# Value moments on ScalarE, routing rows split and sent later, and new orders in three queues of a fused attention and mixture-of-experts kernel

## The reference

```
x = x + mixing(layernorm(x), k, skip, ctx)    # mixing, per row pair (i, j) of a head block of 8 rows:
#   kv = v_i * x2_j ;  y = causal_conv(kv, k_head) + kv * skip_i ;  out_j = sum_i y_ij * x1_i   (x1 = x2 = ctx)
x = x + ffn(layernorm(x))
#   ffn: scores = sigmoid(xf @ gate.T); top 2, weights normalised, times 2.5
#   shared = (silu(xf @ sg.T) * (xf @ su.T)) @ sd.T     (hidden width 704)
#   routed = sum over the 2 experts of weight * ((silu(xf @ eg.T) * (xf @ eu.T)) @ ed.T)   (hidden width 352)
```

## Time and profile before

| | |
|---|---|
| median of 3 runs | 714.75 us (713.62 to 715.01) |
| the profiled execution | 712.94 us, of which the trace spans 710.9 us |
| TensorE busy | 654.9 us, 92% of the span |
| VectorE, ScalarE, GpSimd busy | 447.6, 294.1, 352.3 us |
| mean granted TensorE clock | 0.979 |

### The profile page before, as it was taken

The page is one execution under the profiler, slowest core; times in us unless marked ns, Lnnn a source line. Parts: engine busy times, 40 slices in busy tenths (PEclk is TensorE's granted clock), DMA queues, the critical chain, the costliest instruction groups (busy, mean ns, idle before and its releaser), DMA issues.

```text
span 710.9 us, 11541 instructions
## 1 busy us (share of the span) xinstructions
PE 654.9 (92%) x3475; PEld 330.8 (47%) x3476; DVE 447.6 (63%) x720; ACT 294.1 (41%) x374; POOL 352.3 (50%) x294
## 2 busy tenths in 40 slices
PE   5979878977999999899999998996999999999993
PEld 3534334433444444344444443444555555555551
DVE  5999988876987695988896778873432111221110
ACT  5356679333233643233541277623433332323321
POOL 2999899926676355685565006400132223222322
PEclk9999999999899999999999999999999999999998
...
GB/s 206 289 108 116 93 89 148 23 50 48 107 102 92 177 30 16 101 65 62 88 30 125 256 177 304 353 149 171 224 167 130 131 125 137 132 133 124 143 73 58
DMA packets 130519, 91.57 MB, mean 129 GB/s; under 512 B 96992, under 2 KB 110816, under 8 KB 129952
## 3 DMA queue, kind: packets, MB, share of 16 engines
...
q10 hardware_dynamic: 576, 0.82, 0.5%
...
## 4 chain that ended last, share of the span: by engine, by line
PE 55%; DVE 15%; POOL 10%; ACT 8%; issue 4%; DMA 3%; SPq 3%; POOLq 0%; DVEq 0%; ACTq 0%
PE banks L809 16%; PE banks L810 16%; PE banks L811 16%; POOL arena L655 7%; DVE mixT L1462 2%; PE banks L901 2%; DVE arena L1455 2%; DVE stats L1468 2%; POOL arena L712 1%; PE banks L905 1%; PE banks L906 1%; POOL arena L683 1%; DMA arena<-split_filters 1%; DVE silu L1497 1%; DVE hm L1602 1%
## 5 line engine op out<-in xcount | busy, mean ns | idle before, releaser
L655 POOL TENSOR_TENSOR arena<-arena 128x512 f32<-128x512 f32 x120 | 140.4, 1200 | 58.8 <-ACT arena L1155 31.5
L772 POOL DMA_INDIRECT out<-xf,ids x39 | 60.7, 1557 | 183.5 <-DMA out<-xf,ids 130.1
L809 PE MATMUL banks<-arena 128*128 128x512 f16 (+1 forms) x330 | 124.9, 379 | 16.9 <-DVE arena L1455 13.0
L810 PE MATMUL banks<-arena 128*128 128x512 f16 (+1 forms) x330 | 124.9, 379 | 0.0
L811 PE MATMUL banks<-arena 128*128 128x512 f16 (+1 forms) x330 | 124.9, 378 | 0.0
L809 PE MATMUL banks<-arena,normed 128*128 x312 | 97.5, 313 | 0.0
L810 PE MATMUL banks<-arena,normed 128*128 x312 | 97.5, 313 | 0.0
L811 PE MATMUL banks<-arena,normed 128*128 x312 | 97.5, 313 | 0.0
L1817 DVE SCALAR_TENSOR_TENSOR hm<-banks,silu 128x256 f32<-128x256 f32 x39 | 16.5, 424 | 117.3 <-PE banks L811 98.9
L1115 ACT ACTIVATE arena<-arena 128x2048 f16<-128x2048 f32 x31 | 59.0, 1904 | 70.8 <-POOL arena L655 68.1
L1455 DVE TENSOR_TENSOR arena<-banks,arena 128x512 f32<-128x512 f32 x128 | 80.4, 681 | 11.7 <-PE banks L811 11.5
...
## 6 DMA issues: line engine op xcount, KB each, us to landing
...
```

The lines of the kernel that those rows point to most:

```text
L655: nc.gpsimd.tensor_tensor(kv[s % 2][:, lb * COLS:(lb + 1) * COLS].rearrange("p (b j i) -> p b j i", i=NH, j=NH), v[:, a, None, :].to_broad ...
L772: nc.gpsimd.indirect_dma_start(out=out, out_offset=bass.IndirectOffsetOnAxis(ap=ids[slot][:, 0:1], axis=0), in_=yg[slot], in_offset=None, ...
L809: nc.tensor.matmul(dst, wh, xh, start=(k == 0), stop=False)
L810: nc.tensor.matmul(dst, wh, xl, start=False, stop=False)
```

## The change

Edits, by queue:

1. **Value moments** leave VectorE. ScalarE makes them with its accumulator: four Copy instructions (scale -1/L) for minus the mean, four Square instructions (bias minus the mean) for the variance. `value_root` on GpSimd does three instructions of 128x4 (scale and add, power, product). `values` on ScalarE reads new tiles for scale and bias.
2. **Head 11's low part** goes from VectorE to GpSimd.
3. **GpSimd's order in group 1**: `outer` 10 to 13 and low parts 10, 11, 12 come in a block, pieces 6 and 7 behind low part 12.
4. **Pair rows**: `pairs` is split in `pair_ranks` (next to head 6) and `pair_rows` (head 7). `send_rows(g-2)` goes behind `outer(s0+2)` of group g, instead of the end of group g-1; the last but one is sent behind the loop.
5. **ScalarE's order**: filter 11 is turned ahead of `feed_norm(0)`, high part 12 after the shared pieces; in groups 1 and 2 `gated` stands ahead of `high_parts` at h=6; `values` between the two parts of `gated(.., 2)`.
6. **VectorE's order in group 1**: two tiles of `mixed(0)` ahead of `products(8)`, the other two behind `total(8)`, and the rest interleaved.
7. **SyncE**: filter 13 is loaded ahead of the rows of group 2; in the tail the first four `load_ids` go ahead of the loads of expert 6, and the loads of experts 6 and 7 come one tile later.
8. **Tail**: in the last group's hidden tiles VectorE's pieces of experts 1 and 3 are spread over m=1 to 4 (`between`), ScalarE does `gated_high` first and its two pieces behind, waiting for expert 1's low parts; `pieces_behind` moves one tile later for most pieces.
9. **TensorE**: in group 2 both halves of `prepare(3)` stand behind head 21.

```
-DVE_LOWS = (0, 1, 3, 5, 6, 7, 8, 9, 11) + tuple(range(2 * HG - 2, H, 2))
+DVE_LOWS = (0, 1, 3, 5, 6, 7, 8, 9) + tuple(range(2 * HG - 2, H, 2))
...
-        pieces_behind = {1: [(6, 0), (6, 1)], 2: [(6, 2)], 3: [(6, 3)]} | {c + 4: [(7, c)] for c in range(EX_PARTS)}
+        between = {1: [(1, 2), (1, 3)], 2: [(3, 0), (3, 1)], 3: [(3, 2)], 4: [(3, 3)]}
+        loads_behind = {1: (6, 2), 2: (6, 3), 3: (7, 0), 4: (7, 1), 5: (7, 2), 6: (7, 3)}
+        pieces_behind = {1: [(6, 0), (6, 1)], 3: [(6, 2)], 4: [(6, 3)]} | {c + 5: [(7, c)] for c in range(EX_PARTS)}
...
# SyncE, g == 1
                 load_filter(s0 + 4)
                 if g == 1:
+                    load_filter(s0 + 5)
                     sp.wait_ge(shared_l, 7)
# SyncE, tail
             load_tile(3, 3)
+            for t in range(RING):
+                load_ids(t, t)
             load_expert(6, 0, 1)
...
                 if t == 0:
-                    for u in range(RING):
-                        load_ids(u, u)
                     sp.wait_ge(base_ready, Q * G)
...
-                if t < 2:
-                    load_expert(6, t + 2)
-                elif t < 2 + EX_PARTS:
-                    load_expert(E - 1, t - 2)
+                if t in loads_behind:
+                    load_expert(*loads_behind[t])
...
# GpSimd
+            def value_root(g):
+                pool.wait_ge(value_square_ready, Q * g)
+                nc.gpsimd.tensor_scalar(value_var[:], value_square[:], 1 / L, EPS, ALU.mult, ALU.add
+                                        ).then_inc(value_var_ready, 1)
+                pool.wait_ge(value_var_ready, g)
+                nc.gpsimd.tensor_tensor(value_rstd[:], value_var[:], minus_half[:], ALU.pow).then_inc(value_rstd_ready, 1)
+                pool.wait_ge(value_rstd_ready, g)
+                nc.gpsimd.tensor_tensor(value_shift[:], value_mean[:], value_rstd[:], ALU.mult).then_inc(v_shift_ready, 1)
...
-                    low_parts(s0 + h)
+                    if g == 1 and h < 4:
+                        if h == 0:
+                            outer(s0 + 2)
+                            piece(5)
+                            outer(s0 + 3)
+                            inverse_root(1)
+                            low_parts(s0 + 2)
+                            low_parts(s0 + 3)
+                            outer(s0 + 4)
+                            outer(s0 + 5)
+                            low_parts(s0 + 4)
+                            piece(6)
+                            piece(7)
+                        continue
+                    if g != 1 or h > 4:
+                        low_parts(s0 + h)
...
                     if s0 + h + 2 < H:
                         outer(s0 + h + 2)
+                    if g > 1 and h == 0:
+                        send_rows(g - 2)
                     if g == 0 and h == 2:
-                        inverse_root(1)
+                        value_root(1)
                     elif g > 0 and h == 1:
-                        inverse_root(2 * g)
-                    elif 0 < g < G - 1 and h == (5 if g == 1 else 4):
-                        inverse_root(2 * g + 1)
+                        inverse_root(g)
+                    elif 0 < g < G - 1 and h == 5:
+                        value_root(g + 1)
...
-                else:
-                    send_rows(g - 1)
-            inverse_root(2 * G - 1)
+            send_rows(G - 2)
+            inverse_root(G)
...
# ScalarE
+            def value_moments(g):
+                act.wait_ge(x_in[g], 32)
+                act.wait_ge(skip_ready, Q * g)
+                act.wait_ge(tokT_ready, Q * g)
+                for q in range(Q):
+                    nc.scalar.activation(normed[:, q, :], x_tok[g % 3][:, q, :], ACT.Copy, scale=-1 / L,
+                                         accum_out=value_mean[:, q:q + 1]).then_inc(value_mean_ready, 1)
+                act.wait_ge(value_mean_ready, Q * g)
+                for q in range(Q):
+                    nc.scalar.activation(normed[:, q, :], x_tok[g % 3][:, q, :], ACT.Square, bias=value_mean[:, q:q + 1],
+                                         accum_out=value_square[:, q:q + 1]).then_inc(value_square_ready, 1)
...
# ScalarE, h == 5 and h == 6 of groups 1 and 2
                         turn_filter(s0 + h + 1)
-                        if g == 1:
-                            values(g + 1)
+                        gated_silu(g - 1, 2)
+                        values(g + 1)
+                        gated_high(g - 1, 2)
                         high_parts(s0 + h + 2)
-                        gated(g - 1, h - 3)
...
                         turned(g + 1, range(2, Q))
+                        gated(g - 1, h - 3)
                         high_parts(s0 + h + 2)
-                        gated(g - 1, h - 3)
...
                         gated(g - 1, h - 3)
-                        if 1 < g < G - 1 and h == 4:
-                            values(g + 1)
+                        if 0 < g < G - 1 and h == 4:
+                            value_moments(g + 1)
...
# VectorE, g == 1
+                    mixed_tile(0, 0)
+                    mixed_tile(0, 1)
+                    products(s0, 0, g)
+                    dve.wait_ge(outT_ready, Q)
+                    total(s0, 0)
+                    mixed_tile(0, 2)
+                    mixed_tile(0, 3)
+                    mixed_moments(0)
+                    mixed_moments(0, True)
+                    products(s0 + 1, 1, g)
+                    mixed_shift(0)
+                    total(s0 + 1, 1)
+                    feed_low(0, range(0, 2))
+                    products(s0 + 2, 2, g)
+                    feed_low(0, range(2, Q))
+                    total(s0 + 2, 2)
...
-                    if h == (6 if g < G - 1 else 4):
+                    if g == G - 1 and h == 4:
                         pairs(g - 1)
+                    elif g < G - 1 and h == 6:
+                        pair_ranks(g - 1)
+                    elif g < G - 1 and h == 7:
+                        pair_rows(g - 1)
```

114 lines of the change are left out of this document (55 added, 59 removed).

## The result

The changed kernel takes 723.26 us (median of 4, 721.39 to 725.05), the kernel before in the same session 714.88 us (median of 4, 713.62 to 716.54). The ratio is 1.0116 with a 95% interval of 1.0082 to 1.0149: slower by 1.2%. The forecast was 707.3 us, with a range of 699.5 to 716 us.

What follows compares the result with a forecast made beforehand. The prediction took TensorE, busy 92% of the span, to bound the kernel, so only closing its gaps or keeping its clock up pays. Nine terms summed to -7.4 us, from the median 714.75 to 707.3 us, range 699.5 to 716.

Steps and rivals of the forecast that it cites:

- 1 group 0: Group 0: convolve(3) starts sooner without VectorE's moments, but GpSimd's queue gives the gain back; 0 us (-1.3 to +1.6).
- 2 front of group 1: Group 1 up to convolve(13): one gap moves to convolve(10), another goes, later work slips; -0.7 us (-3 to +2).
- 3 rest of group 1: Group 1 from convolve(13): earlier values and silu(0,3) close gaps and low clock, pair_rows costs some; -9.3 us (-12 to -5).
- 4 entry of group 2: Entry of group 2: row transfers ahead of low part 17, outer(19) and the root delay the root; +4.2 us (+1 to +7).
- 5 inside of group 2: Inside group 2: gaps at convolve(20), near 286 us and at 301.2 us go; -3.4 us (-3.4 to 0).
- 6 entry of group 3: Entry of group 3: root 4 us later, but meets some 3 us of spare time; +1 us (0 to +3).
- 7 last hidden tiles: Last hidden tiles: later silu(3,2) and pieces between products make down(3,0) wait for VectorE; +3.7 us (0 to +4.5).
- 8 hidden layer of tile 1: Transfer at 496.7 us: ids and a load leave the queue between turns, so the wait goes; -7.0 us (-7.0 to -4).
- 9 ahead of tile 9: Ahead of tile 9: VectorE's 28th piece comes a tile later, TensorE waits; +3.3 us and +0.8 for the clock.
- Dear moments: Rival: ScalarE's accumulating instructions take 1.3 us each, with activation table loads; +4.6, 719.4 us, slower; chance 0.13.
- The root behind the transfers: Rival: the late root makes the entries of groups 2 and 3 cost 7 and 5 us; -0.6, 714.2 us; chance 0.10.
- more is gained: Rival: last-hidden-tiles and tile 9 costs are hidden, group 1's first gaps close too; -14, 700.7 us; chance 0.19.

Runs made afterwards that it cites:

- e16: e9 with var_eps in a two-operand form and pair rows behind products(15) and its total in groups 1 and 2; 710.43 us.
- e11: Changed kernel with the row transfers in two halves around the root, behind outer(19); 733.41 us.
- e15: e9 with var_eps in a two-operand form and low part 17 ahead of the row transfers in GpSimd's queue; 714.30 us.
- e18: Changed kernel with VectorE's add_shared(0) ahead of the second half of the moments in groups 2 and 3; 718.52 us.
- e9: Changed kernel with group 1's front, last hidden tiles and last pieces as before, and expert loads one tile earlier, ids kept ahead; 711.03 us.
- e6: Changed kernel with the front of group 1 (queue orders, low part 11, filter 13) as before; 717.20 us.
- e8: Changed kernel with ScalarE's high part 16 (24) ahead of silu(0,3) in head 6 of groups 1 and 2, as before; 730.09 us.
- e5: Changed kernel with pair ranks and pair rows together in head 6 and row transfers at the end of the group, as before; 722.03 us.
- e7: Changed kernel with the value moments back on VectorE, every queue order as changed; 733.27 us, ratio 1.0228.
- e3: Changed kernel with SyncE's order behind the tiles and the places of the pieces of experts 6 and 7 as before; 720.46 us.
- e4: Changed kernel with expert loads one tile earlier and last pieces in their old places, ids still ahead of the first turn; 717.06 us.

## Why the prediction was wrong

Its terms against the starts of TensorE, in us:

| term | forecast | trace | |
|---|---|---|---|
| 1 group 0 | 0 | -0.6 | right |
| 2 front of group 1 | -0.7 | +3.4 | outside its bounds |
| 3 rest of group 1 | -9.3 | -8.1 | right |
| 4 entry of group 2 | +4.2 | +6.4 | size within bounds, cause wrong for TensorE |
| 5 inside of group 2 | -3.4 | +0.5 | outside its bounds |
| 6 entry of group 3 | +1 | +2.3 | within bounds |
| 7 last hidden tiles | +3.7 | +4.4 | right |
| 8 hidden layer of tile 1 | -7.0 | -7.2, then +5.6 | first half came |
| 9 ahead of tile 9 | +4.1 | +5.6 | right, within bounds |
| sum (forecast) and start of tile 10 (trace) | -7.4 | +12.4 | |

- **The step that failed is what pair rows and the other small instructions around the root cost on VectorE (terms 4 to 6: +1.8 forecast, +9.2 found).** I took pair rows at the 3.5 us that they last before, as +0.8 us once in group 1, and put the entry down to the root behind the transfers. The runs show that VectorE's small instructions last as long as GpSimd lets them: pair rows 2.3 us beside an idle GpSimd (e16), 5.5 beside `outer`, 9.0 beside `outer` and a low part (e11, e15); var_eps 0.17 us beside an idle one (e11) and 2.7 to 5.2 us beside a run in group 2. The end of `pick(1)` went from 0.85 to 3.3 us the same way. The change moved work on GpSimd to just these places. The root did come late: the transfers took 15.9 us instead of 13.6, the root ended 27.1 us behind `outer(18)` instead of 23.2, and VectorE waited 1.84 us for it where it waited 0 before. But no gap of TensorE above 0.9 us follows from that; the one at `down(0,2)` stands ahead of it, behind var_eps. How much of the 9.2 us is VectorE's held instructions is not isolated: moving `add_shared` out from behind var_eps returned 1.8 us at `convolve(17)` (e18), and every kernel that left GpSimd idle beside one of the two places paid elsewhere. Why a small instruction stays held over several of GpSimd's is not shown; in group 3 var_eps was held for one only, 1.06 us in the changed kernel and 1.03 us in e9, with three more of GpSimd's behind.
- **Term 2** named each wait and mis-sized their sum. I had the gap move to `convolve(10)` at about the size of the one it replaced; it is 4.04 us and brings 5.3 us at the low clock with it, and filter 12, issued behind the transposes, lands at 121.5 us, so that low part 12 and the two pieces come late on GpSimd. e6 puts the whole at 5.2 us, the later kernels at 3.4 to 6.5.
- **Term 3** held by its place and size. Without the order in head 6 the stretch loses 4.9 us (e8), without pair rows in head 7 5.0 us (e5), without ScalarE's moments 1.7 us (e7; the forecast gave them 0.9 us). That the order pays only with pair rows in head 7 was not in the forecast, which counted pair rows as a cost alone. The moments are worth more elsewhere: e7 is 4.1 us late already at `convolve(13)` and 11.0 us at the start of group 3.
- **Term 5** forgot pair rows in group 2 (1.74 us at `convolve(24)`), and the gap at `convolve(20)`, which it had go, is 1.95 us. The step that failed fails here too: the moments left VectorE, and the small instructions of `pick(1)` and one low part, held beside GpSimd now, took 3.2 us more.
- **Term 8** was right in that its wait went, and the ids are what decides over it (e3 and e4). Part of that was luck: the last hidden tiles held tile 0 back by 3.5 us, and in the kernels where they don't, with the loads of before, 1.9 to 2.8 us of the wait stay. It missed 5.6 us at the next tile, a wait that comes in 4 of 9 traces with that order. **Term 9** was right in place and cause (e4); the wait was 4.34 instead of 3.3 us and the clock 1.7 instead of 0.8 us. Of the 19.8 us between forecast and trace at tile 10, terms 4 to 6 make 7.4, term 8 5.4 and term 2 4.1.
- **The rivals.** Dear moments fall: 0.61 and 0.71 us each, no table load; on ScalarE they are a gain, 8.0 us by the ratio of e7. The Trainium skill (ScalarE: Activation LUTs, Table sets: the hidden batching unit) left Square's set open; this trace shows no load in front of it. The root behind the transfers was the rival nearest to what happened, in its place and not in its mechanism, and alone would not have made it slower. The rival "more is gained" says that terms 7 and 9 are hidden but subtracts only term 7; with both, its own sum is -18.2 and 696.5 us. No rival had the new front as a loss.

Both forms of var_eps were held, 3.41 us with one operand and 3.07 us with two. The Trainium skill (SBUF — State Buffer, Who interferes with whom) says that VectorE and GpSimd share a pair of ports and that whichever issues first holds it for its whole instruction while the other is blocked; it counts VectorE's instructions with two inputs in SBUF among these, and copies and one-operand forms in a fast mode. By that rule the traces agree that both forms can be blocked. They differ in length: var_eps waited not for one instruction of 1.1 us but to the end of a run of up to four, while each held instruction of pair rows waited for one. In the prediction I used the rule only in the direction of a held GpSimd.
